# One expert layer of a four-layer decoder: by blocks of routed rows instead of all experts for all tokens

## The reference, cut to what matters

```python
scores = jnp.einsum('td,ed->te', xt, gate_w)
probs = jax.nn.softmax(scores, axis=-1)
expert_weights, expert_indices = jax.lax.top_k(probs, TOP_K)
expert_weights = expert_weights / expert_weights.sum(-1, keepdims=True)
x1 = jax.nn.silu(jnp.einsum('ti,eoi->teo', xt, w1))
x3 = jnp.einsum('ti,eoi->teo', xt, w3)
expert_outs = jnp.einsum('teo,eio->tei', x1 * x3, w2)
sel = jnp.take_along_axis(expert_outs, expert_indices[:, :, None], axis=1)
out = jnp.einsum('tai,ta->ti', sel, expert_weights)
```

## Time and profile before

| what | value |
|---|---|
| median of 3 runs | 1449.04 us (1448.42 to 1449.28) |
| profiled execution | 1452.28 us |
| its span, first to last instruction | 1450.6 us |
| mean granted TensorE clock | 0.891 |
| PE busy / DVE busy / ACT busy / POOL busy | 1195.1 / 987.1 / 703.2 / 282.0 us |

### The profile page before, as it was taken

How to read it: one execution, slowest core, us unless ns; L and a number is a source line. 1 busy time by engine, 2 the same in 40 slices (tenths; PEclk the granted TensorE clock), 3 DMA queues, 4 the chain that set the end, 5 groups by cost and what they waited for, 6 DMA issues and landing times. The chain is left out here.

```text
span 1450.6 us, 24473 instructions
## 1 busy us (share of the span) xinstructions
PE 1195.1 (82%) x8092; PEld 798.2 (55%) x8092; DVE 987.1 (68%) x2547; ACT 703.2 (48%) x1507; POOL 282.0 (19%) x395
## 2 busy tenths in 40 slices
PE   6766777789888988997586669999958999888898
PEld 4222343457575745684243346788835767664566
DVE  3997775666787776547268887533368999845555
ACT  4443566555434456653255435422235556545553
POOL 3455122001111010012021100000015445311000
PEclk7886798799999988998699678999988999999899
DMA  6004222013312130134422100210000001032111
GB/s 202 29 0 130 76 81 78 20 60 91 115 56 78 45 122 12 60 93 161 155 68 78 63 31 24 77 30 23 1 16 1 2 1 31 19 106 64 59 64 40
DMA packets 69066, 89.23 MB, mean 62 GB/s; under 512 B 5960, under 2 KB 52048, under 8 KB 67152
## 3 DMA queue, kind: packets, MB, share of 16 engines
q1 hardware_dynamic: 68944, 87.67, 18.8%
HBM read 63.46 MB, written 23.72 MB: 60 GB/s over the span
## 5 line engine op out<-in xcount | busy, mean ns | idle before, releaser
L1297 ACT ACTIVATE P<-bank 128x512 f32<-128x512 f32 (+1 forms) x448 | 229.5, 596 | 112.4 <-PE bank L1022 95.8
L1646 DVE TENSOR_REDUCE mx<-bank 128x2 f32<-128x512 f32 x320 | 195.0, 684 | 63.1 <-PE bank L998 63.1
L1097 PE MATMUL bank<-xT,room 128*128 128x256 f32 x640 | 167.6, 396 | 0.4
L1457 POOL TENSOR_SCALAR rstd<-mv 128x2 f32<-128x2 f32 x56 | 13.9, 248 | 766.3 <-DVE mv L1508 662.8
L1106 PE MATMUL bank<-room 128*128 128x256 f32 x640 | 162.5, 392 | 0.0
L1097 PEld LDWEIGHTS bank<-xT,room 128*128 128x128 f32 x640 | 122.5, 197 | 23.5 <-issue 4.7
L1035 PE MATMUL bank<-P,V 128*32 128x256 f32 (+1 forms) x1536 | 123.2, 450 | 12.6 <-ACT P L1297 11.1
L1106 PEld LDWEIGHTS bank<-room 128*128 128x128 f32 x640 | 121.8, 196 | 20.9 <-issue 3.6
L1022 PE MATMUL bank<-QKR 50*128 50x256 bf16 (+1 forms) x896 | 85.5, 288 | 44.1 <-DVE mx L1646 14.7
L998 PE MATMUL bank<-QKR 48*128 48x256 bf16 (+1 forms) x896 | 83.5, 299 | 36.2 <-ACT P L1297 8.5
L1785 DVE TENSOR_TENSOR room<-bank,room 128x512 f32<-128x512 f32 x64 | 44.2, 691 | 93.9 <-PE bank L1097 93.8
(11 more groups left out here) (231 smaller groups left out, 2307.0 us busy)
## 6 DMA issues: line engine op xcount, KB each, us to landing
QKR<-split_rows SPq DMA_DIRECT2D x112, 192.0 KB
room<-gate_rows SPq DMA_DIRECT2D x64, 256.0 KB, 3.8
split_rows<-parts SPq DMA_DIRECT2D x56, 192.0 KB, 2.3
split_rows<-parts SPq DMA_DIRECT2D x56, 128.0 KB, 1.9
room<-in_w SPq DMA_DIRECT2D x6, 1024.0 KB, 7.3
room<-in_w SPq DMA_DIRECT2D x3, 2048.0 KB, 14.4
split_rows<-parts SPq DMA_DIRECT2D x56, 64.0 KB, 1.7
room<-in_mask SPq DMA_DIRECT2D x4, 512.0 KB, 4.4
```

The source lines that it names most:

```text
L1097: last = nc.tensor.matmul(bk[:, j * S:(j + 1) * S], w[:, e, (2 * f + j) * 128:(2 * f + j + 1) * 128], x, start=True, stop=True)
L1297: nc.scalar.activation(P[:, (e - 1) % NBUF_P, 0:width], psum(st, p)[:, 0:width], ACT.Exp, scale=SCALE).then_inc(read[k], 1)
L1646: V_.reduce_max(to, sc[:, :].rearrange("p (t s) -> p t s", t=TPB), AX.X).then_inc(read[k], 1)
```

## The change

MoE 2 becomes a dispatch for two batches (a pair, 512 tokens, 1024 routed rows) at a time:

- GATE keeps the one-hots of both picks. SLOT counts the rows of each expert with small matmuls (a triangular one and ones), rounds each expert up to blocks of 128 rows, and gives each routed row a slot and each of the 15 blocks an expert number.
- SC scatters the token rows by 8 indirect DMAs of POOL for a pair (4 tiles, 2 picks) to `slots_in` in HBM, which was filled with zeros at the start. BL loads 3 blocks at a time, and BT transposes them.
- EID loads 15 expert numbers into registers of PE. For each of the 15 blocks: DH and DG, one matmul of 512 columns each, whose weight address comes from the register; silu on ACT; the product on DVE; DX, four transposes and an ACT copy; DO, four matmuls of 128 columns into 128 output features, with an address from the register, and an ACT copy.
- YS stores 3 blocks to `slots_out`; YG gathers them by 8 indirect DMAs of POOL for a pair; STAT adds each of the two rows times its gate to x (four DVE instructions).
- The number of blocks is fixed at 15 for a pair, whatever the routing.
- XG, MG, GB, GL, BI, MO, YC and YT of MoE 2 are gone. The linear attention now waits for the last DO, and its first LT also for the last YS.

Beside it, GATE writes the gates of both tiles and both picks with whole-tile instructions in all MoE layers, part of them while the exp runs. The exp of MB is a step of its own (MX) over all 512 columns, MC is a lane of its own, and the scan is two instructions of 256 columns. COST, LANDING, MOST and FAVOUR have other values and PIPE is new, so that `plan` gives another order. Some semaphores are shared.

```diff
+DISPATCHED = 2
+NBLOCK, NGROUP, PER_GROUP = 15, 5, 3
...
+PIPE = 0.2
...
-MOST = {"score": 4, "prob": 4, "up": 1, "mamba": 5, "out": 5, "feat": 2, "turn": 2, "mix": 3}
+MOST = {"score": 4, "prob": 4, "up": 1, "mamba": 3, "out": 5, "feat": 5, "turn": 2, "mix": 4}
...
     if k in ("GQ",):
-        return x_of(SUB_OF[("attn", GATHERED)], r[0]) + [("MO", 2, B - 1, NE - 1, 1)]
+        return x_of(SUB_OF[("attn", GATHERED)], r[0]) + [("DO", 1, NBLOCK - 1)]
...
+    if k == "SC":
+        return [("SLOT", r[0]), ("LD", "zero")]
+    if k == "BL":
+        pair, g = r
+        i = NGROUP * pair + g - 2
+        return [("SC", pair, t) for t in range(2 * TPB)] + ([("BT", i // NGROUP, i % NGROUP)] if i >= 0 else [])
...
+    if k == "YG":
+        pair, t = r
+        return [("YS", pair, g) for g in range(NGROUP)] + [("STAT", SUB_OF[("moe", DISPATCHED)], t // TPB) if pair else ("SPLIT", MASKED, B - 1)]
...
+                elif k == "EID":
+                    pe.wait_ge(slots_done, 2 * st[1] + 2)
+                    _, expert = nc.values_load_multi_w_load_instructions(expert_at[0:1, 16 * st[1]:16 * st[1] + NBLOCK], engines=[mybir.EngineType.PE], min_val=0, max_val=NE - 1,
+                                                                         skip_runtime_bounds_check_because="a sum of seven comparisons")
...
+                elif k in ("DH", "DG"):
+                    pair, j = st[1:]
+                    if block_no(st) == 0:
+                        pe.wait_ge(experts_in, EXPERTS_IN[DISPATCHED])
+                    finished(pe, ("BT", pair, j // PER_GROUP))
+                    w = (w1s[DISPATCHED] if k == "DH" else w3).rearrange("p e f -> p (e f)")
+                    x = blockT[:, (NGROUP * pair + j // PER_GROUP) % 2, j % PER_GROUP * D:(j % PER_GROUP + 1) * D]
+                    last = nc.tensor.matmul(bk[:, :], x, w[:, bass.DynSlice(expert[j] * 512, 512)], start=True, stop=True)
+                elif k == "DX":
+                    i = block_no(st)
+                    finished(pe, ("DG", *st[1:]))
+                    for c in range(4):
+                        last = nc.tensor.transpose(bk[:, c * 128:(c + 1) * 128], gated_in[:, i % 2, c * 128:(c + 1) * 128], ident[:, :])
+                elif k == "DO":
+                    pair, j = st[1:]
+                    finished(pe, ("DX", pair, j))
+                    w = w2s[DISPATCHED].rearrange("p e c d -> p (e c d)")
+                    for c in range(4):
+                        last = nc.tensor.matmul(bk[:, 0:D], gatedT[:, block_no(st) % 2, c * 128:(c + 1) * 128], w[:, bass.DynSlice(expert[j] * 512 + c * 128, 128)],
+                                                start=(c == 0), stop=(c == 3))
...
-                    later, steps_in = (x.rearrange("p (b s) -> p b s", s=S)[:, :, 1:S] for x in (abar[:, i % 2, :], dt[:, 512 * c:512 * (c + 1)]))
-                    nc.scalar.activation(later, steps_in, ACT.Exp, scale=negA[:, n:n + 1]).then_inc(abar_done, 1)
+                    nc.scalar.activation(abar[:, i % 2, :], dt[:, 512 * c:512 * (c + 1)], ACT.Exp, scale=negA[:, n:n + 1]).then_inc(abar_done, 1)
...
+                elif k == "SC":
+                    _, pair, t = st
+                    pool.wait_ge(lin_loaded, 16 * N_LIN + 32)
+                    pool.wait_ge(slots_done, 2 * pair + 1)
+                    if pair:
+                        pool.wait_ge(scattered, 16 * 4 * TPB)
+                    for w in range(2):
+                        at = 8 * pair + 2 * t + w
+                        nc.gpsimd.indirect_dma_start(slots_in[pair], bass.IndirectOffsetOnAxis(ap=slot_at[:, at:at + 1], axis=0),
+                                                     x_tok[:, 2 * TPB * pair + t, :], None).then_inc(scattered, 16)
+                elif k == "YG":
+                    _, pair, t = st
+                    for r in range(2):
+                        pool.wait_ge(blocks_out[r], 16 * sum(i % 2 == r for i in range(NGROUP * (pair + 1))))
...
+                        nc.gpsimd.indirect_dma_start(back[:, t, w, :], None, slots_out[pair],
+                                                     bass.IndirectOffsetOnAxis(ap=slot_at[:, at:at + 1], axis=0)).then_inc(back_in[t // TPB], 16)
...
-                    V_.tensor_tensor_scan(hs[:, (i - 1) % 2, :], abar[:, (i - 1) % 2, :], bu[:, (i - 1) % 2, :], 0.0, ALU.mult, ALU.add).then_inc(scan_done, 1)
+                    for b in range(2):
+                        part = slice(b * S, (b + 1) * S)
+                        last = V_.tensor_tensor_scan(hs[:, (i - 1) % 2, part], abar[:, (i - 1) % 2, part], bu[:, (i - 1) % 2, part], 0.0, ALU.mult, ALU.add)
+                    last.then_inc(scan_done, 1)
...
+                        for w in range(2):
+                            for t in range(TPB):
+                                V_.scalar_tensor_tensor(out=r[:, t, :], in0=back[:, b % 2 * TPB + t, w, :], scalar=gates[:, TPB * b + t, w:w + 1],
+                                                        in1=r[:, t, :] if w else x[:, t, :], op0=ALU.mult, op1=ALU.add).then_inc(dve_chain, 1)
...
-                    for t in range(TPB):
-                        g = gates[:, TPB * b + t, :]
-                        link(V_.tensor_scalar(g, iota[:, 0:NE], top_atf[:, t, 0:1], gs[:, t, 0:1], ALU.is_equal, ALU.mult))
-                        link(V_.tensor_scalar(gtmp[:, :], iota[:, 0:NE], top_atf[:, t, 1:2], gs[:, t, 1:2], ALU.is_equal, ALU.mult))
-                        link(V_.tensor_tensor(g, g, gtmp[:, :], ALU.add))
...
-                    V_.tensor_copy(gtmp[:, :], gtmp[:, :]).then_inc(gates_done, 1)
+                    link(V_.tensor_tensor(picks, picks, gs[:, :, 0:2].unsqueeze(3).to_broadcast([128, TPB, 2, NE]), ALU.mult))
+                    V_.tensor_tensor(gates[:, TPB * b:TPB * (b + 1), :], picks[:, :, 0, :], picks[:, :, 1, :], ALU.add).then_inc(gates_done, 1)
...
+                elif k == "SLOT":
+                    pair = st[1]
+                    full(dve, st)
+                    link(V_.tensor_scalar(scaled_count, bk[:, 32:40], 1.0 / 128, None, ALU.mult))
+                    link(V_.tensor_tensor(over, scaled_count.unsqueeze(2).to_broadcast([128, NE, 4]), iota[:, 0:4].unsqueeze(1).to_broadcast([128, NE, 4]), ALU.is_gt))
+                    link(V_.reduce_sum(filled_blocks, over, AX.X))
+                    link(V_.tensor_tensor_scan(upto, ones[:, 0:NE], filled_blocks, 0.0, ALU.mult, ALU.add))
+                    link(V_.tensor_tensor(first, upto, filled_blocks, ALU.subtract))
```

523 lines of the change are left out of this document (321 added, 202 removed), and 3 rows, old and new, of the table UNITS.

## The result

The kernel after takes 1386.18 us, the median of 4 runs (1382.51 to 1390.83), against 1448.73 for the one before on the same chip (4 runs, 1447.68 to 1449.28): a ratio of 0.9571, with a 95% interval of 0.9541 to 0.9601. On another chip it was 0.9559 (0.9528 to 0.9590). So the change takes off 62.5 us, and 1394 was 8 us too high, inside the likeliest case's own range.

What follows compares the result with a forecast made beforehand. The prediction took PE to bound MoE 2 and DVE the linear attention. Its terms, -54 + 7 - 6 + 3 - 5 = -55 us, taken from the median 1449.04, gave 1394 us, range 1360 to 1425.

Steps and rivals of the forecast that it cites:

- the likeliest case: The forecast itself, 1394 us for the whole kernel, own range 1380 to 1408, chance 0.56.
- Parts 1 to 4: MoE 2's dispatch up to the linear attention: 44 us gained after the last GATE, together 54 us.
- Part 1: PE's work in MoE 2: 30 blocks at 3.3 us replace 64 units of 2.59 us; register addresses 0.05 a block.
- Part 2: Last GATE to pair 1's first block: slots, 8 scatters at 1.3 us, landing, load and transposes, 19 us.
- Part 3: Up to the last GATE: pair 0's blocks run beside attention; last GATE 10 us earlier (0 to 21.6).
- The sign that I named for "wrong": In MoE 2, pair 0's blocks not done before pair 1 is ready: a PE backlog of up to 20 us.
- Part 5: Linear attention takes on pair 1's 8 gathers (+3) and STAT and NORM of batches 2 and 3 (+4): +7 us.
- Part 6: GATEs outside MoE 2 -6 us (0 to -19), scans +3 (-3 to +6), order -5 in the ramp, zero elsewhere.
- 1, slow blocks: MoE 2 blocks slower than 3.3 us, by register arithmetic stalling PE or its lower clock: 1417 us, chance 0.10.
- 2 and 3, a dear indirect DMA: An indirect DMA costs POOL about 2.2 us (1416 us, chance 0.10) or the full 3.8 (1454 us, chance 0.04).
- 4, the attention gives more: Last GATE comes 20 us earlier and the order finds 12 us in idle shares: 1372 us, chance 0.18.
- 5: The gain in MoE 2 is wholly used up by waits elsewhere: 1449 us, chance 0.02.

Runs made afterwards that it cites:

- all but the dispatch: Kernel before with whole-tile gates, MX apart, split scans and new planner values, MoE 2 still dense: 1441.69 us, ratio 0.9970.
- the second execution: Profiled execution of the unchanged kernel after on another chip, span 1376.8 us; median there 1379.76 us, ratio 0.9559 to the kernel before.
- the first execution: Profiled execution of the unchanged kernel after on the first chip: 1386.95 us, with a span of 1385.2.
- the slower POOL: Kernel after with four small chained POOL memsets beside each indirect DMA: 1392.43 us, ratio 0.9640 to the kernel before.
- DH preferred less: Kernel after with one planner preference changed, DH of MoE 2 at 0.6 instead of 3.6: 1391.21 us, ratio 0.9612 to the kernel before.
- the order alone: Kernel before with only the planner values of the kernel after (COST, LANDING, MOST, FAVOUR, PIPE): 1455.10 us, ratio 1.0061.
- the scans' row: Stage times of the kernel before with only two scans of 256 columns and the exp over 512: 1445.52 us, ratio 0.9988.
- the other way: Kernel after with the old planner values (1400.30 us, ratio 0.9701), read against the kernel before with whole-tile GATE alone (1434.56 us, ratio 0.9912).

## Why the prediction came out as it did

The forecast's mechanism was right: MoE 2 was bound by PE, and the gain is the PE work that the dispatch takes off behind the last GATE. Its largest term came out right as a sum, of pieces that were not; the small terms were wrong in size or sign and partly cancelled.

**Parts 1 to 4, the dispatch (-54).** Measured between "all but the dispatch" and the second execution: 54.0 us between masked bias and LV; against the first it is 48.0. That the 54 agrees to the microsecond is partly luck: of the 54.0, 48.2 lie behind the last GATE, where I had 44 (120.7 there without the dispatch, for my 114.7), and 5.7 ahead of it, where I had 10. In pieces, last GATE to first LV: forecast 70.5, measured 77.8 in the first execution, with its pause of some 2.7 us, and 72.5 in the second, of which 20.7 for 19 and 51.8 for 51.5.
- Part 1, the block: 3.05 us, 3.16 with BT, where I had 3.3. I had taken DX with its pipeline's end (0.51), and in the dense stretch that end lies under the next group: 0.44. BT's third is 0.11 and not 0.13, and the address arithmetic nothing where I had 0.05. That takes 2 us off 15 blocks. Against it stand two places: the start, where the lower clock costs some 2.7 us (above), and one distance of 4.45 us between two silus in place of 3.05 (952.42 and 956.87 in the second execution), where pair 0's STAT and NORM stand in DVE's queue ahead of DG's product and PE's transposes wait for NORM.
- Part 2, the chain to the first block, in the second execution: 4.4 us to POOL's first indirect DMA (I had 2.7), 9.9 for the scatters (10.4), 1.3 to the load's issue (2.3), 2.6 for the load (2.6), 2.5 for BT with its copy (1.1). 20.7 for 19. In the 4.4, SLOT's small DVE instructions up to the slots take 2.0 as I had it; PE's six tiny matmuls hold them off for 1.7 and not 0.7; and 0.8 pass between the slots and the first indirect DMA, for which I had no term. With the slower POOL the first memset starts 0.1 us after the slots (919.49 against 919.38), so POOL was free to go, and the 0.8 seems to be the indirect DMA's own. In the 2.5, 1.0 is the load of the expert numbers, which I had held to be hidden, and BT of two groups at the lower clock the rest.
- Part 3: I held pair 0's 15 blocks to be PE load up to the last GATE, and took 10 us. Counted from masked bias it is 169.1 - 159.4 = 9.7, but counted from the start of the causal attention, as I had put it, 292.6 - 288.5 = 4.1 (5.4 in the second execution), just below the 5 to 15 of my sign. Only 11 of the blocks stand there.
- The sign that I named for "wrong", pair 0's blocks not done when pair 1 is ready, was there in the first execution and cost some 3.3 us (the estimate above). In the second, pair 0 is done before pair 1's rows are there. With DH preferred less it is the bound, and costs 10 us.

**Part 5, the linear attention (+7).** Measured +7.6 and +5.4 from LV to the last LY, but not by the terms given, and the sum agrees partly by luck. The gathers (+3) cost nothing: they are issued from 996.2 to 1006.0, and POOL's first product of LS starts at 1014.1. STAT and NORM of batches 2 and 3 (+4) are dearer, 7.3 us of DVE. Their rows, with POOL's product beside them, from the kernel after:

```profile
1011.19 0.61 DVE L1756 SCALAR_TENSOR_TENSOR res<-qk,gates,res 128x128 f32<-128x128 f32 x2
...
1014.08 3.81 POOL L1643 TENSOR_TENSOR room<-room,lden 128x1024 f32<-128x1024 f32 x2 [0.35 <-DVE lden L1993]
...
1015.28 2.75 DVE L1756 SCALAR_TENSOR_TENSOR res<-qk,gates,x_tok 128x128 f32<-128x128 f32 x2
```

Two instructions that take 0.61 us together elsewhere take 2.75 and end 0.14 us after POOL's products do. One of the two is held for each of POOL's two products: their own records end at 1016.13 and 1018.03, 0.15 and 0.14 us after a product's. And the +7 doesn't belong to the dispatch: without it the new order alone has +9.5 there, and under the new order the dispatch has -4.5. DVE's busy time in this stage is 210.7 us before and 217.4 with the order alone, for the same 334 instructions, so the order makes the same work longer there; what holds it wasn't followed.

**Part 6.** Three terms:
- GATE -6, for the twelve GATEs outside MoE 2; with the gates' part of Part 3 I had some -8 for all sixteen. Measured -12.7 for all sixteen. I had spread 19 us of DVE work over DVE's busy share, a third; of the 23 us that go, 55% turned into time. The instructions are linked, and SLOT, SC, GB and the next expert units wait for their end, so a share above DVE's own is what one would expect; that this is the reason was argued and not tested, and it isn't the whole length either. How much of the miss lies in the twelve can't be told, since the profile has 9.4 us ahead of the causal attention, where the scans' row moves by 6 without a cause.
- Scans +3: measured none; the second start is 0.05 us, and the last scan starts at 121.2 us after and 121.8 before.
- Order -5: measured +9 on the work of before and -20.5 on that of after. The size had bounds of -25 and +15, and what came lies near both and past neither. The 5 us that I took back in the ramp didn't come: LV to first LY is 95.5 before, 99.4 with the order alone and 104.4 after, though DVE idles 3 us less. The gain is ahead of the causal attention, where I had written zero.

With my signs: dispatch -47 (with Part 5) for -59, gates -6 for -13, scans +3 for -2 (none within its interval), order -5 for +9, and -55 for -64 in all by ratio on the second chip (-62.5 on the first). The dispatch's own miss of 12 us lies behind the first LV: -4.5 and -4.5 where I had +7. The -4.5 in the rest I didn't follow. The split holds for this way from before to after alone; by the other way the dispatch is -31 and the new order -20.5.

**The rivals.** 1, slow blocks: the register half is refuted by 3.05 us a block with fixed addresses too. The clock half happened in the second execution, as it was put: PE waited for the first block and started pair 1 at the lower level, but for 6.8 us only, which costs some 2.7 us where the whole rival had 23; the clock was 1.00 from 939.6 to the linear attention. 2 and 3, a dear indirect DMA: refuted by 1.26 us an issue, in each of the 32 scatters and gathers (their medians are 0.958 and 0.944 us, and 0.30 lies between two). The Trainium skill's page SBUF — State Buffer, section "A bandwidth-pool intuition that's wrong", has the descriptors of such a DMA wait until a DVE copy releases the port, 3.1 us in place of 0.62; here no issue took over 1.24 us, though DVE was busy for 8.7 of the 9.8 us of pair 1's gathers, with reductions and products that read a bank; so this trace doesn't show it for such instructions. 4, the attention gives more: in part, since the early stages gave 27.6 us, but by the order and the gates and not by pair 0's blocks. 5: refuted.

## What to carry to other kernels

Small linked instructions for which other engines wait can be worth more than their engine's busy share: here 55% of the work taken off showed, and the share was a third. A list of preferences written by hand is fitted to its work: the same order was worth +9 us on one kernel and -20 on its successor, so a change and its order are judged together, and each stage by itself. When a backlog and a chain of transfers end close to each other, the bound can change from one execution to the next: with a pause of 2.7 us it was the backlog, and without it eight indirect DMAs at 1.26 us each, which shortening the one and lengthening the other showed.

## What the hardware showed that I had not expected

- An indirect DMA of 128 rows of 512 bytes holds POOL 0.94 to 0.96 us (1.00 to 1.24 for the first of a series) and leaves 0.30 us to the next, the same for scatters and gathers. Its first record of a series starts 0.8 to 0.9 us after the slots are known.
- Matmuls with addresses from registers run as fast as with fixed ones (3.05 us a block in both). Each address has a register instruction of 46 to 60 ns in PE's sequencer, 180 in all, and the load of 15 expert numbers takes 1.58 to 1.77 us of it, twice; in front of pair 1's first block it costs some 1.0 us.
- A scan over 256 columns takes 0.66 to 0.69 us alone, and two behind each other 1.9 where POOL's product runs beside them, as one over 512 does.
- DVE's 128-column scalar_tensor_tensor on SBUF, 0.35 us, takes 1.98 when POOL's product over 1024 columns runs. DVE's reduction over 1024 columns beside the same product took its usual 1.2 us. The Trainium skill's page SBUF — State Buffer, section "Who interferes with whom", says that a DVE instruction with two inputs in SBUF contends with a GpSimd instruction that reads SBUF; the row at 1015.28 agrees.
- TensorE's clock was 0.78 of its upper level in the 101 us up to the last GATE, where it had been 0.92, with PE's work down from 87 to 70 us. What that took back of the lighter load wasn't priced.
